# Feed-forward tiles in pairs: the orders of VectorE, ScalarE and GpSimd written anew over a whole pair, no operation moved between engines

## The chip, the cores and the metric

The kernel is one program on one core of a Trainium2 chip. Its metric is the device time of that core in microseconds. Engines are named as in the profile: PE is TensorE's matmul, PEld its weight load, DVE is VectorE, ACT ScalarE, POOL GpSimd, SP SyncE, which issues most DMAs. "L953" is line 953 of the kernel.

## What is computed

The input x is 4 x 2048 rows of 256. Three layers follow each other: half a feed-forward layer, causal attention with one head, and the same feed-forward layer again:

```python
x = x + 0.5 * ffn(layernorm(x), w_gate, w_up, w_down)
x = x + attention(layernorm(x), Wq, Wk, Wv)
x = x + 0.5 * ffn(layernorm(x), w_gate, w_up, w_down)

def fp4_linear(x, w):                      # einsum('bsk,nk->bsn')
    return fp4_quant_dequant(x) @ fp4_quant_dequant(w).T
def ffn(x, w_gate, w_up, w_down):          # inner width 704
    h = silu(fp4_linear(x, w_gate)) * fp4_linear(x, w_up)
    return fp4_linear(h, w_down)
```

`fp4_quant_dequant` takes blocks of 16 elements: scale = max|x| / 6, x / scale is rounded to the grid 0, 0.5, 1, 1.5, 2, 3, 4, 6 with its sign, and multiplied by the scale. It is applied to x (256 wide) and to h (704 wide), for every row. Attention is softmax over the scaled, causally masked scores, 2048 keys.

## The kernel before

The 8192 rows are 64 tiles of 128 rows, which stay in SBUF (`x_sb`). A feed-forward stage runs over 32 pairs of tiles; with `NP` = 32, a pair is `gp`, its tiles are 2 gp (`u` = 0) and 2 gp + 1 (`u` = 1). In the prediction they are called a and a+1. Between the two feed-forward stages lies attention. The order of every engine is written out by hand, as one function per engine that emits one pair (`pe_pair`, `dve_pair`, `act_pair`, `pool_pair`, `sp_pair`); loops repeat them, with pairs unrolled at both ends of a stage. Engines meet through semaphores that count tiles or pairs. Every engine works strictly in its order, and a wait holds up all that stands behind it.

What is done for a tile n of h, with the helpers' names and lines:

- TensorE: `pe_gate_up` (L1456, 18 matmuls) makes gate and up in PSUM for tile n, then `pe_down` (L1417, 17 matmuls) the down product of tile n-4. Before a gate and up product it waits for h of tile n-2, before a down product for the landing of the transposed codes of its tile and for the residual add two tiles back.
- ScalarE: `act_silu` (L708), `act_h_n` (L715, cells of the scaled h), `act_h_c` (L721, codes), `act_h_fc` (L725, a factor per row).
- VectorE: `dve_h` (L953, up times silu), `dve_h_amax` (L957, maxima of blocks), `dve_h_s` (L962, scales), `dve_h_rin` (L966, their reciprocals), `dve_h_max`, `dve_h_pow`, `dve_h_inv` (L970, L974, L979: one value per row), `dve_h_sp` (L984, scaled scales), `dve_h_sd`, `dve_h_sh`, `dve_h_sl` (L988, L992, L996: the scale split in a high and a low half), `dve_h_g` (L1001, rounding), `dve_h_q` (L1009, both code planes), `dve_res` (L1019, residual add, four tiles behind).
- GpSimd: `pool_h_y` (L540), h times the reciprocals of `dve_h_rin`.
- SyncE: `sp_h_T` transposes the code planes by DMA.

For a pair of x tiles, two to four pairs ahead: row statistics on ScalarE (`act_x_mean` L669, `act_x_squares` L681) and GpSimd (`pool_x_rstd`, three instructions of two elements, L515, L519, L521), normalised x (`act_x_z`, L693), and the same quantization: `dve_x_amax` L902, `dve_x_s` L907, `dve_x_rin` L911, `dve_x_sd`, `dve_x_sh`, `dve_x_sl` (L915, L919, L923), `pool_x_y` L529, `act_x_n` L702, `act_x_c` L730, `dve_x_g` L931, `dve_x_q` (L942, twice), and the transposition `sp_x_T`.

In `dve_pair` before, the body is a loop over u: each half begins with `dve_h_rin(n)`, then come h_max, the residual add, h_pow, h and h_amax of the next tile, h_inv, h_sp, h_q of the tile before, and the splitting of the scales. The x steps of pair gp+2 stand in the first half, those of gp+3 in the second. At the start of the second feed-forward stage two attention adds (`dve_last_add`, L1123, L1125, L1129) are still to be done; the stage's first down product waits for them (`o_add`), since it writes the PSUM bank that they read.

## Time and profile before

| | us |
|---|---|
| median of 3 runs | 1306.32 |
| lowest, highest | 1304.23, 1306.85 |
| the profiled execution | 1305.19 |
| its span, first to last instruction | 1303.4 |
| PE busy in the span | 1165.0 (89%) |
| DVE busy | 1054.2 (81%) |
| ACT busy | 786.9 (60%) |
| POOL busy | 568.9 (44%) |

The profile is of one execution; its span lacks 1.8 us of its time. Busy time counts an instruction from its start to its end, with what it waits for inside, so a group with a longer mean than its work explains is worth a look. The shares are means over stages: the first feed-forward stage runs from about 50 to 450 us, attention to about 920, and the second feed-forward stage to the end. In the timeline, "[0.35 <-issue]" is idle time of the engine before the instruction, and what ended it. TensorE's granted clock is 0.99 of full speed.

### The profile page before, as it was taken

Reading aid. Unit: us, or ns where it says so; the run is one execution under the profiler, and the core shown is the slowest. Engines: PE = TensorE matmul, PEld = TensorE weight load, DVE = VectorE, ACT = ScalarE, POOL = GpSimd, SP = SyncE. Lnnn points to the kernel's source line nnn. Section 1 sums busy time; section 2 is a strip of 40 time slices with the busy share of each in tenths; the row PEclk is TensorE's granted clock in tenths of the full one; section 3 lists DMA queues with packets and bytes.
Section 4 is the critical chain, followed back from the end, with each engine's and each line's share of the span. In section 5 each row is a group of like instructions: output and inputs, shape, how many; then the busy total and the mean of one; then the engine's idle time right before and its main releaser. Section 6 shows DMA issues by size and latency. Waiting matters only on the chain.

```text
span 1303.4 us, 25349 instructions
## 1 busy us (share of the span) xinstructions
PE 1165.0 (89%) x7673; PEld 746.1 (57%) x7673; DVE 1054.2 (81%) x3257; ACT 786.9 (60%) x1663; POOL 568.9 (44%) x531
## 2 busy tenths in 40 slices
PE   2689998998998789989998999989999889889897
PEld 1255555555554556666675667556665555555555
DVE  6899999999999766547555655664899999999997
ACT  4667777667764345435533543565676776776763
POOL 2444444544544244434442453444354454444442
PEclk9899999999999999999999999999999999999999
DMA  6953443444444546655663665556254454544545
GB/s 213 228 103 72 84 86 73 88 81 79 83 80 73 105 93 118 99 114 96 110 122 79 117 97 121 91 97 113 55 105 102 104 107 96 107 103 96 112 100 126
DMA packets 462743, 134.41 MB, mean 103 GB/s; under 512 B 441296, under 2 KB 461904, under 8 KB 462672
## 3 DMA queue, kind: packets, MB, share of 16 engines
q1 hardware_dynamic: 454928, 125.62, 50.1%
q10 hardware_dynamic: 7744, 7.86, 1.9%
q8 instruction: 42, 0.69, 0.2%
q14 instruction: 29, 0.24, 0.1%
HBM read 11.34 MB, written 8.39 MB: 15 GB/s over the span
## 4 chain that ended last, share of the span: by engine, by line
DVE 34%; PE 26%; issue 23%; ACT 8%; POOL 6%; DMA 1%; SPq 1%; ACTq 1%; DVEq 1%; POOLq 0%
PE ps L1503 11%; PE ps L1491 8%; DVE arena L953 5%; DVE arena L1009 5%; DVE arena L957 4%; POOL arena L540 3%; PE ps L1456 3%; POOL arena L529 2%; PE ps L1476 2%; DVE arena L1113 2%; DVE arena L966 2%; ACT arena L669 2%; PE ps L1469 1%; ACT arena L781 1%; DVE arena L942 1%
## 5 line engine op out<-in xcount | busy, mean ns | idle before, releaser
L1456 PE MATMUL ps<-wguT,arena 128*128 128x512 f16 (+1 forms) x2304 | 480.3, 363 | 5.7 <-DMA arena<-arena 5.6
L1456 PEld LDWEIGHTS ps<-wguT,arena 128*128 128x128 f16 x2304 | 225.9, 98 | 227.0 <-issue 10.3
L540 POOL TENSOR_TENSOR arena<-arena 128x704 f32<-128x704 f32 x128 | 192.0, 1500 | 368.3 <-DVE arena L966 368.3
L1417 PE MATMUL ps<-wdT,arena 128*128 128x256 f16 x2176 | 263.0, 275 | 73.1 <-DMA arena<-arena 69.4
L1417 PEld LDWEIGHTS ps<-wdT,arena 128*128 128x128 f16 x2176 | 209.4, 99 | 128.8 <-issue 74.1
L567 POOL TENSOR_TENSOR arena<-arena 128x128 f16<-128x128 f32 (+7 forms) x64 | 143.9, 2249 | 236.4 <-ACT arena L781 197.1
L715 ACT ACTIVATE arena<-arena 128x704 int16<-128x704 f32 x128 | 100.9, 788 | 167.0 <-POOL arena L540 165.9
L790 ACT ACTIVATE arena<-ps,arena,cst 128x128 f16<-128x128 f32 (+7 forms) x64 | 80.5, 1258 | 193.8 <-DVE arena L1118 189.9
L1503 PE MATMUL ps<-arena 128*128 128x256 f16 x1632 | 188.8, 273 | 9.3 <-DVE x_sb L1129 9.3
L1491 PE MATMUL ps<-arena 128*128 128x512 f16 (+3 forms) x960 | 187.7, 348 | 3.5 <-ACT arena L781 3.5
L1503 PEld LDWEIGHTS ps<-arena 128*128 128x128 f16 x1632 | 158.0, 98 | 37.0 <-DVE x_sb L1129 9.1
L1491 PEld LDWEIGHTS ps<-arena 128*128 128x128 f16 x960 | 91.2, 98 | 91.3 <-ACT arena L781 4.5
L953 DVE SCALAR_TENSOR_TENSOR arena<-ps,cst,arena 128x704 f32<-128x704 f32 x128 | 120.8, 944 | 23.1 <-issue 14.4
L1100 DVE SCALAR_TENSOR_TENSOR arena<-ps,arena 128x512 f16<-128x512 f32 x64 | 44.0, 691 | 98.7 <-ACT arena L773 98.7
L957 DVE TENSOR_REDUCE arena<-arena 128x44 f32<-128x704 f32 x128 | 113.4, 886 | 4.4
L708 ACT ACTIVATE arena<-ps,cst 128x704 f32<-128x704 f32 x128 | 106.6, 833 | 14.4 <-PE ps L1456 8.8
L1009 DVE TENSOR_TENSOR arena<-arena 128x1408 f16<-128x1408 f16 x128 | 113.4, 886 | 0.6 <-issue 0.3
L1113 DVE TENSOR_REDUCE arena<-ps 128x1 f32<-128x512 f32 (+3 forms) x160 | 95.2, 607 | 16.6 <-PE ps L1491 14.4
L721 ACT ACTIVATE arena<-arena 128x704 f16<-128x704 int16 x128 | 99.8, 779 | 0.4
L529 POOL TENSOR_TENSOR arena<-arena 128x512 f32<-128x512 f32 x64 | 69.6, 1087 | 55.5 <-DVE arena L911 55.5
L781 ACT ACTIVATE arena<-ps,arena,cst 128x128 f32<-128x128 f32 (+7 forms) x64 | 80.0, 1251 | 9.9 <-POOL arena L567 9.9
L1129 DVE SCALAR_TENSOR_TENSOR x_sb<-ps,arena,x_sb 128x256 f32 (+1 forms) x64 | 31.0, 484 | 58.3 <-PE ps L1503 53.7
(128 smaller groups left out, 1510.2 us busy)
## 6 DMA issues: line engine op xcount, KB each, us to landing
out_dram<-x_sb SPq DMA_DIRECT2D x32, 256.0 KB, 2.7
x_sb<-in_L_attn_x_dram ACTq DMA_DIRECT2D x3, 2048.0 KB, 8.7
arena<-arena SPq DMA_TRANSPOSE x384, 3.5
arena<-arena SPq DMA_DIRECT2D x8, 256.0 KB, 3.3
arena<-arena SPq DMA_DIRECT2D x4, 512.0 KB, 3.3
x_sb<-in_L_attn_x_dram ACTq DMA_DIRECT2D x1, 1536.0 KB, 7.3
arena<-in_L_ffn_w_down_dram SPq DMA_DIRECT2D x1, 704.0 KB, 8.8
arena<-in_L_ffn_w_gate_dram SPq DMA_DIRECT2D x1, 640.0 KB, 4.5
```

The costliest lines, as they stand in the source:

```text
L540: g.tensor_tensor(hy[u].rearrange("p (j b) -> p b j", j=BL), h[u].rearrange("p (b j) -> p b j", j=BL), hri[u].unsqueeze(2).to_broadcast([P ...
L567: nc.gpsimd.tensor_tensor(pq[k][1][:, 0:w], prob[:, 0:w], pq[k][0][:, 0:w], ALU.subtract).then_inc(p_lo, 1)
L708: nc.scalar.activation(sg[u], ps_gate[u], ACT.Silu, scale=cst[:, C_G:C_G + 1]).then_inc(h_silu, 1)
L715: nc.scalar.activation(hn[u], hy[u], ACT.Copy, scale=CELLS, bias=-0.5).then_inc(h_n, 1)
L953: V.scalar_tensor_tensor(h[u], ps_up[u], cst[:, C_U:C_U + 1], sg[u], ALU.mult, ALU.mult).then_inc(h_h, 1)
L957: V.tensor_reduce(ham[u], h[u].rearrange("p (b j) -> p b j", j=BL), axis=AX.X, op=ALU.max, apply_absolute_value=True).then_inc(h_amax, 1)
L1009: V.tensor_tensor(hq[u].rearrange("p (l j b) -> p l j b", l=2, j=BL), hc[u].rearrange("p (j b) -> p j b", j=BL).unsqueeze(1).to_broadcast( ...
L1113: m = V.tensor_reduce(scmax[:, c:c + 1], ps_s[:, c0 + c * GW:c0 + end], axis=AX.X, op=ALU.max)
L1417: i = nc.tensor.matmul(ps_dn[w % 2], hT[w][:, c * P:(c + 1) * P], wdT[:, k, :], start=(s == 0), stop=(s == len(DOWN_STEPS) - 1))
L1456: i = nc.tensor.matmul(psf[:, 1536 * u + lo:1536 * u + hi], xv[:, u, xl, kt, :], wguT[:, wl, lo // P:hi // P, kt, :], start=(s == 0), stop ...
L1491: m = nc.tensor.matmul(ps_s[:, c0:c0 + w], y[:, k, yl, qc:qc + P], zT[:, k, zl, k0:k0 + w], start=(s == 0), stop=(s == KT * 3 - 1))
L1503: m = nc.tensor.matmul(ps_o, pT[color(i)][pl][:, k, :], vs[:, vt, vl, :], start=(s == 0), stop=(s == len(steps) - 1))
```

## The change

The same operations are issued by the same engines. `dve_pair` no longer has a loop over u but one list for both tiles; `act_pair` and `pool_pair` are written anew too. `pool_x_rstd` is split in three functions so that its parts can stand apart. Two waits are added: `act_h_fc(n)` for the residual add of tile n-4, and `dve_h_pow(n)` for `act_h_fc(n-2)`. TensorE's and SyncE's orders are as before. The two attention adds of the second stage's second pair stand at new places.

```diff
         def pool_pair(gp, odd, x3=True, x4=True, z1=False):
             pool_h_y(2 * gp, 0)
+            if x4:
+                pool_x_var(gp + 4, odd)
             if z1:
                 pool_z_lo(1)
             pool_h_y(2 * gp + 1, 1)
+            if x4:
+                pool_x_root(gp + 4)
+                pool_x_shift(gp + 4, odd)
             if x3:
                 pool_x_y(gp + 3)
-            if x4:
-                pool_x_rstd(gp + 4, odd)
...
         def act_h_fc(n, u, w):
             nc.scalar.wait_ge(h_pw, n + 1)
+            if not isinstance(n, int) or n >= 4:
+                nc.scalar.wait_ge(res, n - 3)
...
         def act_pair(gp, p, odd, start=None, x2=True, x3=True, x4=True, z1=False):
+            a = 2 * gp
+            act_silu(a, 0)
+            if x4:
+                act_x_mean(gp + 4, p + 4, odd)
+            if start != 0:
+                act_h_n(a - 1, 1)
+                act_h_c(a - 1, 1)
+            act_silu(a + 1, 1)
...
+            if x2:
+                act_x_n(gp + 2)
+            if start != 0:
+                act_h_fc(a - 1, 1, (2 * odd - 1) % 4)
+            if x4:
+                act_x_squares(gp + 4, p + 4, odd)
+            if x2:
+                act_x_c(gp + 2)
+            if x3:
+                act_x_z(gp + 3, p + 3)
+            act_h_n(a, 0)
+            act_h_fc(a, 0, 2 * odd)
+            act_h_c(a, 0)
...
         def dve_h_pow(n, u):
             V.wait_ge(h_mx, n + 1)
+            if not isinstance(n, int) or n >= 2:
+                V.wait_ge(h_fc, n - 1)
...
+            a = 2 * gp
+            dve_h_rin(a, 0)
+            dve_h_max(a, 0)
+            dve_h(a + 1, 1)
+            if start is None:
+                dve_res(a - 4, 2 * odd, p * 2 - 4)
+            if adds:
+                dve_last_add(TB - 2)
+            dve_h_pow(a, 0)
+            dve_h_amax(a + 1, 1)
+            if start != 0:
+                dve_h_q(a - 1, 1, quad(qd, 2 * odd - 3))
+            if x2:
+                dve_x_sh(gp + 2)
+            dve_h_s(a + 1, 1)
+            if x2:
+                dve_x_sl(gp + 2)
+            dve_h_inv(a, 0)
+            dve_h_rin(a + 1, 1)
+            if x2:
+                dve_x_g(gp + 2)
+            dve_h_max(a + 1, 1)
+            dve_h_sp(a, 0)
+            if x3:
+                dve_x_amax(gp + 3)
+            if not end:
+                dve_h(a + 2, 0)
+            if x3:
+                dve_x_s(gp + 3)
+            dve_h_sd(a, 0)
+            if x2:
+                dve_x_q(gp + 2, 0, (qd + odd, 1 - odd))
+                dve_x_q(gp + 2, 1)
+            if x3:
+                dve_x_rin(gp + 3)
+            dve_h_pow(a + 1, 1)
+            if not end:
+                dve_h_amax(a + 2, 0)
+            dve_h_inv(a + 1, 1)
+            if start is None:
+                dve_res(a - 3, 2 * odd + 1, p * 2 - 3)
+            if adds:
+                dve_last_add(TB - 1)
+            dve_h_sp(a + 1, 1)
+            dve_h_sh(a, 0)
+            dve_h_sd(a + 1, 1)
+            dve_h_g(a, 0)
+            if not end:
+                dve_h_g(a + 1, 1)
+            dve_h_sh(a + 1, 1)
+            dve_h_sl(a, 0)
+            dve_h_sl(a + 1, 1)
+            dve_h_q(a, 0, quad(qd, 2 * odd - 2))
+            if not end:
+                dve_h_s(a + 2, 0)
+            if x3:
+                dve_x_sd(gp + 3)
```

**VectorE in the steady loop, where the second tile's reciprocals are made.** In the changed kernel the lines are higher by 22 to 24: L966 is L988, L970 is L992, L984 is L1008, L902 is L924, L907 is L929, L953 is L975, L931 (x_g) is now L953. Before, the second half of the pair begins:

```order
L966 RECIPROCAL arena<-arena 128x44
L901 REGISTER_ALU
L902 TENSOR_REDUCE arena<-arena 128x32
L970 TENSOR_REDUCE arena<-arena 128x1
L907 TENSOR_SCALAR arena<-arena 128x32
L1016 REGISTER_ALU
L1019 ISA
L1019 SCALAR_TENSOR_TENSOR x_sb<-ps,arena,x_sb 128x256
L911 RECIPROCAL arena<-arena 128x32
L974 TENSOR_SCALAR arena<-arena 128x1
L949 REGISTER_ALU
L953 SCALAR_TENSOR_TENSOR arena<-ps,cst,arena 128x704
```

and in the changed kernel:

```order
L988 RECIPROCAL arena<-arena 128x44
L953 TENSOR_SCALAR arena<-arena 128x512
L992 TENSOR_REDUCE arena<-arena 128x1
L1008 TENSOR_SCALAR arena<-arena 128x44
L923 REGISTER_ALU
L924 TENSOR_REDUCE arena<-arena 128x32
L971 REGISTER_ALU
L975 SCALAR_TENSOR_TENSOR arena<-ps,cst,arena 128x704
L929 TENSOR_SCALAR arena<-arena 128x32
L1012 SCALAR_TENSOR_TENSOR arena<-arena 128x44
```

Behind the reciprocals stood x_amax, h_max and x_s; now stand x_g, h_max and h_sp of the first tile (L1008), and x_s (L929) comes behind x_amax and h.

**VectorE in the second pair of the second feed-forward stage, where the last attention add stands** (three instructions, L1123 to L1129, now L1160 to L1166). Before:

```order
L966 RECIPROCAL arena<-arena 128x44
L902 TENSOR_REDUCE arena<-arena 128x32
L970 TENSOR_REDUCE arena<-arena 128x1
L907 TENSOR_SCALAR arena<-arena 128x32
L1123 RECIPROCAL arena<-arena 128x1
L1125 TENSOR_SCALAR arena<-arena,cst 128x1
L1129 SCALAR_TENSOR_TENSOR x_sb<-ps,arena,x_sb 128x256
L911 RECIPROCAL arena<-arena 128x32
L974 TENSOR_SCALAR arena<-arena 128x1
L953 SCALAR_TENSOR_TENSOR arena<-ps,cst,arena 128x704
```

and in the changed kernel, from h of the stage's tile 4 (L975) on:

```order
L975 SCALAR_TENSOR_TENSOR arena<-ps,cst,arena 128x704
L929 TENSOR_SCALAR arena<-arena 128x32
L1012 SCALAR_TENSOR_TENSOR arena<-arena 128x44
L964 TENSOR_TENSOR arena<-arena 128x2x256 x2
L933 RECIPROCAL arena<-arena 128x32
L998 TENSOR_SCALAR arena<-arena 128x1
L979 TENSOR_REDUCE arena<-arena 128x44
L1003 TENSOR_SCALAR arena<-arena 128x1
L1160 RECIPROCAL arena<-arena 128x1
L1162 TENSOR_SCALAR arena<-arena,cst 128x1
L1166 SCALAR_TENSOR_TENSOR x_sb<-ps,arena,x_sb 128x256
```

The add stood ahead of h (L953); now h (L975) and eight more steps stand ahead of it.

## Rows read from the trace of the kernel before

**Rows 1.** Stage table, two steady stretches: start:end length, busy us (count) per engine, clock, DMA.
```profile
89.07:379.71 290.64, 266.89 (x1701) 164.22 (x1700) 280.00 (x889) 211.34 (x530) 137.09 (x144) 1.00 0.43 81
950.89:1254.30 303.41, 278.19 (x1773) 171.03 (x1771) 292.07 (x927) 220.22 (x550) 142.86 (x150) 1.00 0.49 103
```

**Rows 2.** Timeline of one pair: start, us, engine, line, operation, shape, count [idle before <-releaser].
```profile
202.49 0.29 DVE L931 TENSOR_SCALAR arena<-arena 128x512 int16<-128x512 int16 x1
...
202.89 3.73 PE L1456 MATMUL ps<-wguT,arena 128*128 128x512 f16 x18
...
203.93 0.42 DVE L966 RECIPROCAL arena<-arena 128x44 f32<-128x44 f32 x1
...
204.43 1.49 POOL L540 TENSOR_TENSOR arena<-arena 128x704 f32<-128x704 f32 x1 [4.29 <-DVE arena L966]
...
204.93 1.02 DVE L907 TENSOR_SCALAR arena<-arena 128x32 f32<-128x32 f32 x1
205.77 0.47 DVE L1019 SCALAR_TENSOR_TENSOR x_sb<-ps,arena,x_sb 128x256 f32 x1
...
206.44 0.94 DVE L953 SCALAR_TENSOR_TENSOR arena<-ps,cst,arena 128x704 f32<-128x704 f32 x1
206.46 2.02 PE L1417 MATMUL ps<-wdT,arena 128*128 128x256 f16 x17
...
207.41 0.89 DVE L957 TENSOR_REDUCE arena<-arena 128x44 f32<-128x704 f32 x1
...
208.21 0.14 DVE L979 TENSOR_SCALAR arena<-arena 128x1 int32<-128x1 int32 x1
...
208.31 3.73 PE L1456 MATMUL ps<-wguT,arena 128*128 128x512 f16 x18
208.39 0.25 DVE L984 TENSOR_SCALAR arena<-arena 128x44 f32<-128x44 f32 x1
...
210.48 0.14 DVE L970 TENSOR_REDUCE arena<-arena 128x1 f32<-128x44 f32 x1
210.49 0.83 ACT L708 ACTIVATE arena<-ps,cst 128x704 f32<-128x704 f32 x1
...
211.42 0.95 DVE L953 SCALAR_TENSOR_TENSOR arena<-ps,cst,arena 128x704 f32<-128x704 f32 x1 [0.35 <-issue]
```

**Rows 3.** Line L907 over the whole kernel: minimum/median/maximum ns, first to last start.
```profile
L907 DVE TENSOR_SCALAR arena<-arena x64: 170/1027/1049, 23.7 to 1260.7; 128x32 f32<-128x32 f32 x64
```

**Rows 4.** Timeline, end of the first feed-forward stage, no x_s left.
```profile
436.46 1.49 POOL L540 TENSOR_TENSOR arena<-arena 128x704 f32<-128x704 f32 x1 [1.08 <-DVE arena L966]
...
437.11 0.88 DVE L984 TENSOR_SCALAR arena<-arena 128x44 f32<-128x44 f32 x1
```

**Rows 5.** Timeline, same stage, a GpSimd difference of 1024 columns beside VectorE.
```profile
432.51 2.87 POOL L558 TENSOR_TENSOR arena<-arena 128x1024 f16<-128x1024 f32 x1 [0.97 <-ACT arena L759]
432.51 0.89 DVE L1009 TENSOR_TENSOR arena<-arena 128x1408 f16<-128x1408 f16 x1
433.31 2.13 DVE L988 SCALAR_TENSOR_TENSOR arena<-arena 128x44 f32<-128x44 f32 x1
```

**Rows 6.** Timeline, start of the second feed-forward stage.
```profile
931.41 0.20 DVE L1123 RECIPROCAL arena<-arena 128x1 f32<-128x1 f32 x1
...
931.92 0.48 DVE L1129 SCALAR_TENSOR_TENSOR x_sb<-ps,arena,x_sb 128x256 f32<-128x256 f32 x1
...
934.02 0.95 DVE L953 SCALAR_TENSOR_TENSOR arena<-ps,cst,arena 128x704 f32<-128x704 f32 x1 [1.35 <-PE ps L1456]
...
934.03 2.02 PE L1417 MATMUL ps<-wdT,arena 128*128 128x256 f16 x17
```

**Rows 7.** Lines view, VectorE, 100 to 390 us: busy us, mean ns of one, idle before.
```profile
L942 DVE TENSOR_TENSOR arena<-arena 128x512 f16<-128x512 f16 x48 | 20.2, 421 | 0.0
...
L988 DVE SCALAR_TENSOR_TENSOR arena<-arena 128x44 f32<-128x44 f32 x48 | 9.5, 198 | 0.0
...
L911 DVE RECIPROCAL arena<-arena 128x32 f32<-128x32 f32 x24 | 8.1, 336 | 0.0
```

More of the change, by code:

```diff
@@ L508, in _, with pool_x_var @@
             sp.wait_ge(stored, 16 * NP)
-        def pool_x_rstd(q, par):
+        def pool_x_var(q, par):
             g = nc.gpsimd
@@ L515, in pool_x_rstd, with pool_x_root @@
             g.tensor_tensor(xve, xsq[par], eps_col[:, GT:GT + 2], ALU.add).then_inc(x_ve, 1)
+        def pool_x_root(q):
+            g = nc.gpsimd
             g.wait_ge(x_ve, q + 1)
@@ L519, in pool_x_rstd, with pool_x_shift @@
             g.tensor_tensor(xr, xve, half_neg[:, 0:2], ALU.pow).then_inc(x_rstd, 1)
+        def pool_x_shift(q, par):
+            g = nc.gpsimd
             g.wait_ge(x_rstd, q + 1)
             g.tensor_tensor(xnr, xnm[par], xr, ALU.mult).then_inc(x_nr, 1)
+        def pool_x_rstd(q, par):
+            pool_x_var(q, par)
+            pool_x_root(q)
+            pool_x_shift(q, par)
         def pool_x_y(q):
@@ L732, in act_pair @@
         def act_pair(gp, p, odd, start=None, x2=True, x3=True, x4=True, z1=False):
-            for u in range(2):
-                n, late = 2 * gp + u, start != 0 or u == 1
-                act_silu(n, u)
-                if u == 1 and z1:
-                    act_z_hi(1)
-                    act_load_table(ACT.Exp)
-                if u == 1 and x3:
-                    act_x_z(gp + 3, p + 3)
-                if late:
-                    act_h_n(n - 1, 1 - u)
-                if u == 0 and x2:
-                    act_x_n(gp + 2)
-                if u == 1 and x4:
-                    act_x_squares(gp + 4, p + 4, odd)
-                if late:
-                    act_h_c(n - 1, 1 - u)
-                    act_h_fc(n - 1, 1 - u, (2 * odd + u - 1) % 4)
-                if u == 0 and x2:
-                    act_x_c(gp + 2)
-                if u == 0 and x4:
-                    act_x_mean(gp + 4, p + 4, odd)
+            a = 2 * gp
[6 more added lines that the diff above has]
+            act_silu(a + 1, 1)
+            if z1:
+                act_z_hi(1)
+                act_load_table(ACT.Exp)
+            if x2:
[11 more added lines that the diff above has]
+            act_h_c(a, 0)
         def act_z_hi(g):
@@ L1023, in dve_last_add @@
             dve_attention_add((B - 1) * TB + i, i, ((B - 1) * TB + i) * D)
-        def dve_pair(gp, qd, p, odd, start=None, x2=True, x3=True, end=False, adds=()):
-            for u in range(2):
-                n, v, w = 2 * gp + u, 1 - u, 2 * odd + u
-                k = None if start is None else 2 * start + u
-                early, late = u == 0 and x2, u == 1 and x3
-                more = not (end and u == 1)
-                dve_h_rin(n, u)
-                if late:
-                    dve_x_amax(gp + 3)
-                dve_h_max(n, u)
-                if late:
-                    dve_x_s(gp + 3)
-                if k is None or k >= 4:
-                    dve_res(n - 4, w, p * 2 + u - 4)
-                for i, at_u in adds:
-                    if at_u == u:
-                        dve_last_add(i)
-                if late:
-                    dve_x_rin(gp + 3)
-                dve_h_pow(n, u)
-                if more:
-                    dve_h(n + 1, v)
-                    dve_h_amax(n + 1, v)
-                dve_h_inv(n, u)
-                if early:
-                    dve_x_sh(gp + 2)
-                dve_h_sp(n, u)
-                if k != 0:
-                    dve_h_q(n - 1, v, quad(qd, w - 3))
-                dve_h_sd(n, u)
-                if early:
-                    dve_x_sl(gp + 2)
-                    dve_x_g(gp + 2)
-                if late:
-                    dve_x_sd(gp + 3)
-                if more:
-                    dve_h_s(n + 1, v)
-                dve_h_sh(n, u)
-                if early:
-                    dve_x_q(gp + 2, 0, (qd + odd, 1 - odd))
-                if more:
-                    dve_h_g(n, u)
-                dve_h_sl(n, u)
-                if early:
-                    dve_x_q(gp + 2, 1)
@@ new lines, in dve_pair @@
+        def dve_pair(gp, qd, p, odd, start=None, x2=True, x3=True, end=False, adds=False):
+            a = 2 * gp
[55 more added lines that the diff above has]
+                dve_x_sd(gp + 3)
@@ L1381, in _ @@
                     wv_planes()
-                dve_pair(first + 1, first // 2, 1, 1, start=1, adds=((TB - 2, 0), (TB - 1, 1)) if first else ())
+                dve_pair(first + 1, first // 2, 1, 1, start=1, adds=(first > 0))
                 if not first:
```

## Prediction

> **What bounds the kernel now.** I first read the stage table for the two stretches of steady feed-forward work [rows 1]. The reader is to see that VectorE is busy 572.1 of 594.0 us, TensorE 545.1, ScalarE 431.6 and GpSimd 280.0, at full TensorE clock. The stretches hold 24 and 25 pairs of tiles, so a pair takes 12.12 us. Then I read the timeline of one pair [rows 2]. TensorE needs 3.57 us for a tile's gate and up product (202.89 to 206.46) and 1.85 for a down product (to 208.31): 10.84 per pair, less than the pair takes. VectorE sets the pace, yet it does not work all the time that it is called busy. Three losses stand in the rows:
>
> - **L907, blocked.** dve_x_s has 32 elements, and takes 1.02 us where GpSimd's product L540 (h_y) is under way (204.43 to 205.92); its end falls on that product's end. Over the kernel its shortest is 0.17 us and its median 1.03 [rows 3]. From its start to the next instruction are 0.84 us; unblocked, 0.17 less the overlap of 0.08 that neighbours show leaves 0.10. Loss 0.74 per pair.
> - **L953 of the next even tile** starts at 211.42, 0.10 behind the end of ScalarE's silu L708 (210.49 + 0.83). VectorE is idle for 0.35 before it, and unhindered it would also have had the overlap of 0.08. Loss 0.43.
> - **Back-to-back dependence.** L957 reads what L953 wrote and starts 0.03 behind its end (206.44 + 0.94 against 207.41). Independent neighbours start 0.08 before the end. That is 0.12 lost, twice per pair for L953 and L957, and once for L979 and L984 (208.21 + 0.14, then 208.39). Loss 0.36.
>
> Without them a pair would be 12.12 - 0.74 - 0.43 - 0.36 = 10.59 us of VectorE, below TensorE's 10.84.
>
> **The change, part by part.** No operation is added or removed, so only these losses and new ones count.
>
> *Dependence.* Every pair of dependent neighbours named above gets independent work in between (h_max before h, the residual add and h_pow between h and h_amax; h_inv and h_sp stand apart). All 0.36 go.
>
> *silu.* h of the odd tile now follows h_rin and h_max of the even tile directly, but its silu is issued far ahead: on ScalarE it stands before x_n, x_squares, x_c, x_z and h_n of the next tile. Laying the steps of the timeline end to end in the new order, I estimate that silu(a+1) is done some 3 us before h(a+1), and silu(a+2) 1.4 before h(a+2). The 0.43 go. On TensorE, by the same laying out, down(a) waits about 0.3 us for its transpose and down(a+1) about 0.5 for the residual add, which is placed later; both fit into the 0.8 us that TensorE has spare in a pair of 11.7.
>
> *x_s.* It stands behind x_amax and a whole h (0.54 + 0.86 us) after the product's start, by which time GpSimd is done. The 0.74 go.
>
> *The new stall.* GpSimd's second product, h_y(a+1), starts when h_rin(a+1) ends. In the new order VectorE then has x_g, h_max and h_sp of the even tile. h_sp is L984, and the rows show that it is stopped by the same product: 0.88 us [rows 4] instead of 0.25 [rows 2], ending 0.04 behind the product (436.46 + 1.49 against 437.11 + 0.88). h_y starts 0.08 after h_rin (203.93 + 0.42, then 204.43). h_sp can start only behind x_g (0.29) and h_max (0.14), each less 0.08: 0.18 after h_rin's end. GpSimd is 0.1 ahead. Nor does x_g's holding the port help: when L558 was held off by L1009 (2.87 us for its 1024 columns, both from 432.51), it was GpSimd that went on when L1009 ended, and L988, next in line, took 2.13 us until L558's end [rows 5]. So h_sp is stopped in every pair. Its successor x_amax starts about 0.15 before the product's end, as L1019 did (205.77 against 205.92): 0.08 + 1.50 - 0.15 = 1.43 behind h_rin. Free, it would start at -0.08 + 0.20 + 0.06 + 0.17 = 0.35 (L931's 0.29, L970's 0.14 and L984's 0.25 less 0.08 each). The new stall is 1.08. Its lower bound is 0 (VectorE gets the port first), its upper 1.16 (GpSimd starts 0.08 later, as it does behind some of its waits). I take 1.08, since L540 in the rows starts that way behind the same instruction.
>
> The Trainium skill, "SBUF — State Buffer", section Who interferes with whom, says that VectorE in a two-port mode, or with two SBUF inputs, and a reading GpSimd instruction exclude each other for a whole instruction, and that whoever issues first gets the pair. By that rule too GpSimd comes first here, and the trace agrees: L907 ends 0.03 behind the product.
>
> *The other products.* h_y(a) runs while VectorE does h_max, h, the residual add, h_pow and h_amax, which the rows show running beside L540 or reading PSUM; it ends some 0.4 us before h_q(a-1). x_y ends about when h_sp(a+1) starts: 0 to 0.1. I take 0 for both. x_var, x_root and x_shift act on two elements; split up, they run beside h_amax and h.
>
> *Sum for a pair:* 10.59 + 1.08 = 11.67, so 0.45 saved. It holds in the 49 pairs of the rows and about one more: 50 x 0.45 = 22.5 us.
>
> *Start of the second stage.* The last attention add moves behind h(4), x_s, h_sd, both x_q, x_rin, h_pow, h_amax and h_inv. h(4) starts at 934.02 because its product was late [rows 6]; that stays. From there the steps, each its duration in [rows 2] or [rows 7] less the overlap, are 0.86 + 0.10 + 0.11 + 0.34 + 0.34 + 0.25 + 0.01 + 0.80 + 0.06 = 2.87 (h_pow, of one element, all but vanishes under its neighbours), so the add starts at 936.89 and, taking 0.99 (931.41 to 931.92 + 0.48), ends at 937.88. The stage's first down product, which started at 934.03, waits for it: 3.9 us later, and behind it on TensorE the product of tile 5, whose h comes 3.9 later too. VectorE makes up none of it, since it goes on at 11.67 a pair from there. Cost 3.9, bounds 3 and 4.6.
>
> *Last pairs of each stage.* They have no x_s to gain from, but still the new stall (1.08 in one pair, and h_sd stopped for the rest of a product in the two that follow), against 0.36 saved in each. TensorE covers part of it. The start of the first stage I price at nothing: there is no attention add in it, and its first down product waits for transposed weights. Cost 1 per stage, bounds 0 and 2; together 2.
>
> Sum: -22.5 + 3.9 + 2 = -16.6 us. The profiled execution took 1305.19 us (1.8 outside its span), 1.1 less than the median of 1306.32. From the median: 1289.7; I say **1289**.
>
> **A rule that speaks against the change.** The rows show 0.12 us for each dependent neighbour. The Trainium skill, "VectorE: DVE Perf Modes", section The DRAIN you can't avoid, says that the next instruction waits for an empty pipe anyway and that a semaphore between costs nothing more. By it the 0.36 would not go, and the pair would be 12.03. The rows speak otherwise, so I count 0.36 and keep the rule as a rival.
>
> **The rivals.**
> 1. *VectorE gets the port first.* Then the pair is bounded by TensorE's 10.84: 1.28 x 50 = 64 saved, less 6: about 1248. For it: the race is 0.1 us wide. Against it: the handover to GpSimd in [rows 5]. Chance 0.07.
> 2. *Spacing dependent instructions brings nothing.* Each instruction then costs the same wherever it stands, and the losses are only renamed. Pair 12.03, 50 x 0.09 = 4.5 saved, 5.9 lost: 1307.7, no change. It is also about where the kernel would land if the silu wait stayed (0.43). Against it: the steps in [rows 2]. Chance 0.05.
> 3. *ScalarE's new order is late: slower.* h_fc(a-1) now waits for the residual add of tile a-3, and x_squares, x_c, x_z, h_n and h_c queue behind it. x_g, and with it the second half of the pair, waits for x_c. By my laying out x_c is done about 3.6 us before x_g. From 3.6 us of delay on, every further 0.1 costs 5 us over 50 pairs; at 4.2 the result would be 1289 + 30 = 1319. Against it: ScalarE is busy 8.8 of 12.1 us [rows 1], and the add comes about 0.6 us before h_fc. Chance 0.05.
>
> **How the numbers follow.** The forecast has 0.83. Its own range is 1283 to 1296: 0.08 later starts of h_y give +4, the start and the tails -3 to +3, and the many steps of 0.02 that I left out -3. What is left of the range, 1279 to 1299, is for errors in the count of pairs. It leaves out rival 1 on one side and rivals 2 and 3 on the other, 0.17 in all. A measurement tells 0.2% (2.6 us) from no change. Faster: 0.83 + 0.07 = 0.90; same: rival 2, 0.05; slower: rival 3, 0.05.
>
> **What would show it.** Right: the pairs at 11.6 to 11.75 us; dve_x_s at 0.18 us; h_sp with two forms, about 1.4 to 1.5 us for the even tile of a pair and 0.25 for the odd one; no idle time before h for silu; L953's successor no longer at +0.03; the down product of tile 0 in the second stage near 938. Wrong: h_sp at 0.25 throughout and TensorE without gaps (rival 1); steps between independent neighbours as long as between dependent ones (rival 2); idle time before x_g that ScalarE ends (rival 3); or a product of GpSimd that stops h_q or x_q, which I priced at nothing.

## The result, and the profile after

| | before | after |
|---|---|---|
| median of 7 runs each, us | 1304.23 | 1299.18 |
| lowest, highest | 1303.37, 1306.85 | 1296.09, 1301.17 |
| profiled execution, span | 1305.19, 1303.4 | 1299.57, 1297.7 |

The ratio after to before is 0.9952, 95% interval 0.9938 to 0.9966. The change is faster by 5 us (0.5%), where 17 were forecast. In the changed kernel's page, these lines answer to what the prediction watched: VectorE and TensorE, h, and h_sp.

```profile
PE 1177.7 (91%) x7673; PEld 745.0 (57%) x7673; DVE 1057.6 (81%) x3257; ACT 799.6 (62%) x1663; POOL 522.3 (40%) x531
...
L975 DVE SCALAR_TENSOR_TENSOR arena<-ps,cst,arena 128x704 f32<-128x704 f32 x128 | 121.0, 945 | 21.4 <-PE ps L1493 14.9
...
L1008 DVE TENSOR_SCALAR arena<-arena 128x44 f32<-128x44 f32 x128 | 105.6, 825 | 0.1
```

h_sp (L1008) takes 825 ns in the mean, where the same instruction took 0.25 us in the steady pair of before [rows 2]. The stage table of the changed kernel has the two steady stretches, and then two short ones at the start of the second stage (start:end length, busy us of PE, PEld, DVE, ACT, POOL, clock, DMA):

```profile
91.85:372.45 280.60, 269.08 (x1690) 161.24 (x1687) 280.60 (x890) 219.40 (x533) 117.36 (x144) 1.00 0.46 84
954.50:1246.81 292.31, 280.25 (x1765) 168.78 (x1763) 292.31 (x927) 227.74 (x550) 122.30 (x150) 1.00 0.52 107
928.00:936.00 8.00, 4.08 (x23) 1.99 (x22) 3.88 (x14) 3.11 (x7) 1.06 (x1) 1.00 0.60 114
936.00:943.00 7.00, 7.00 (x36) 3.94 (x35) 2.56 (x12) 0.78 (x2) 1.50 (x1) 0.76 0.34 63
```

The same 24 and 25 pairs as in [rows 1] now take 280.60 and 292.31 us, 11.69 a pair, and VectorE is busy without a break. The forecast for a pair was 11.67. So the steady work is as predicted, and the missing gain is elsewhere. Cut at the same pairs (a pair begins with the reciprocals of its first tile, L966 before and L988 after), the two profiled spans differ like this:

| stretch | before | after | difference |
|---|---|---|---|
| start of the program to pair 3 | 89.07 | 91.85 | +2.78 |
| 24 steady pairs | 290.64 | 280.60 | -10.04 |
| pair 27 | 13.82 | 13.40 | -0.42 |
| pair 28, over attention, to pair 0 of the second stage | 518.73 | 522.58 | +3.85 |
| its pairs 0 to 2 | 38.63 | 46.07 | +7.44 |
| 25 steady pairs | 303.41 | 292.31 | -11.10 |
| the last pairs | 49.08 | 50.93 | +1.85 |
| sum | 1303.38 | 1297.74 | -5.64 |

Steady pairs give 21.6 us, and four short stretches take 15.9 of them back. This is one execution of each kernel. The 24 steady pairs repeat well in the three kernels below that leave them as they are (280.57 to 280.63 us), but the first row does not: of its 2.78, 0.3 stand ahead of the first pair (its reciprocals start at 51.57 before and 51.88 after), and in two kernels below that are the same as the changed one up to there, pair 3 starts at 91.95 and 90.08.

**In a steady pair** the timeline of the changed kernel shows the stall where the prediction put it (an instruction is called stopped when it has started and is held until GpSimd's ends):

```profile
200.76 0.42 DVE L988 RECIPROCAL arena<-arena 128x44 f32<-128x44 f32 x1
...
201.09 0.23 DVE L953 TENSOR_SCALAR arena<-arena 128x512 int16<-128x512 int16 x1
201.24 0.18 DVE L992 TENSOR_REDUCE arena<-arena 128x1 f32<-128x44 f32 x1
201.26 1.51 POOL L554 TENSOR_TENSOR arena<-arena 128x704 f32<-128x704 f32 x1 [2.04 <-DVE arena L988]
201.34 1.46 DVE L1008 TENSOR_SCALAR arena<-arena 128x44 f32<-128x44 f32 x1
...
202.60 0.67 DVE L924 TENSOR_REDUCE arena<-arena 128x32 f32<-128x512 f32 x1
...
203.20 0.93 DVE L975 SCALAR_TENSOR_TENSOR arena<-ps,cst,arena 128x704 f32<-128x704 f32 x1
...
204.06 0.16 DVE L929 TENSOR_SCALAR arena<-arena 128x32 f32<-128x32 f32 x1
...
206.45 0.23 DVE L1008 TENSOR_SCALAR arena<-arena 128x44 f32<-128x44 f32 x1
```

GpSimd's product (L554) starts 0.08 behind the reciprocals, h_sp 0.085 behind that, and it ends 0.04 behind the product. So it is in every steady pair: h_sp starts 83 to 87 ns behind the product. x_amax (L924) starts at 202.60; the odd tile's h_sp takes 0.23. h (L975) has no idle time before it, and x_s (L929) takes 0.16 where it took 1.02 [rows 2].

**At the start of the second stage** the changed kernel's timeline has, for the attention adds and TensorE (L1540 is the product of attention weights and values, L1454 the down product):

```profile
921.15 0.95 DVE L975 SCALAR_TENSOR_TENSOR arena<-ps,cst,arena 128x704 f32<-128x704 f32 x1 [0.97 <-PE ps L1493]
...
922.45 0.48 DVE L1166 SCALAR_TENSOR_TENSOR x_sb<-ps,arena,x_sb 128x256 f32<-128x256 f32 x1
...
923.00 5.41 PE L1540 MATMUL ps<-arena 128*128 128x256 f16 x48 [1.89 <-DVE x_sb L1166]
928.25 3.73 PE L1493 MATMUL ps<-wguT,arena 128*128 128x512 f16 x18
...
932.05 0.95 DVE L975 SCALAR_TENSOR_TENSOR arena<-ps,cst,arena 128x704 f32<-128x704 f32 x1 [4.64 <-PE ps L1493]
...
935.35 0.48 DVE L1166 SCALAR_TENSOR_TENSOR x_sb<-ps,arena,x_sb 128x256 f32<-128x256 f32 x1
...
935.89 2.98 PE L1454 MATMUL ps<-wdT,arena 128*128 128x256 f16 x17 [3.92 <-DVE x_sb L1166]
938.66 4.50 PE L1493 MATMUL ps<-wguT,arena 128*128 128x512 f16 x18
```

Three things stand here. TensorE waits 3.92 us for the last add, as predicted (3.9). It also waits 1.89 for the add before it, which now stands behind an h (921.15) that waits for the end of its gate and up product. And behind the second gap its products are long: 2.98 us where a down product took 2.02 [rows 6], 4.50 where a gate and up product took 3.73 [rows 2]; the granted clock of 936 to 943 is 0.76 of full speed, so a part of that stretch was at 1.2 GHz. In before the same two stretches have 1.00.

**At the start of the first stage** SyncE's issues in before:

```profile
56.91 1.23 SPq L371 DMA_TRANSPOSE arena<-arena  x1
58.24 8.47 SPq L474 DMA_TRANSPOSE wdT<-arena  x6
66.75 3.15 SPq L378 DMA_TRANSPOSE arena<-arena  x2
```

and in the changed kernel:

```profile
59.62 1.23 SPq L371 DMA_TRANSPOSE arena<-arena  x1
60.96 7.89 SPq L474 DMA_TRANSPOSE wdT<-arena  x6
68.89 3.16 SPq L378 DMA_TRANSPOSE arena<-arena  x2
```

L371 transposes the codes that x_q makes of x pair 2. It stands ahead of the last six transposes of the down weights (L474) and of the first h codes (L378) on SyncE's queue. In the new order x_q of pair 2 stands in the second half of pair 0, behind h of the next pair's first tile, so L371 is issued 2.7 us later and L378 2.1, and the first down product starts at 72.67 instead of 70.52. In both kernels it starts 0.13 us behind the landing of the first h codes (70.39 and 72.54); the last down weights had landed 2.3 us before that.

### The profile page after: what moved, and what is told of

Read it like the earlier page. It is cut to its first block, busy times and chain, and to the rows that moved or that the text cites. A ratio compares the mean times of both kernels' runs of the same rounds, so it can differ in the third digit from the quotient of the medians.

```text
span 1297.7 us, 25574 instructions
## 1 busy us (share of the span) xinstructions
PE 1177.7 (91%) x7673; PEld 745.0 (57%) x7673; DVE 1057.6 (81%) x3257; ACT 799.6 (62%) x1663; POOL 522.3 (40%) x531
## 4 chain that ended last, share of the span: by engine, by line
PE 31%; DVE 31%; issue 19%; POOL 7%; ACT 7%; DMA 2%; SPq 2%; ACTq 1%; DVEq 1%; POOLq 0%
PE ps L1540 12%; PE ps L1528 9%; POOL arena L554 6%; DVE arena L1008 6%; PE ps L1493 5%; PE ps L1454 3%; ACT arena L725 2%; DVE arena L1150 2%; PE ps L1513 2%; DVE arena L1025 2%; DVE arena L924 2%; DVE arena L964 2%; DVE x_sb L1043 2%; PE ps L1506 1%; DMA arena<-arena 1%
## 5 line engine op out<-in xcount | busy, mean ns | idle before, releaser
L554 POOL TENSOR_TENSOR arena<-arena 128x704 f32<-128x704 f32 x128 | 192.9, 1507 | 327.7 <-DVE arena L988 327.7
L1454 PE MATMUL ps<-wdT,arena 128*128 128x256 f16 x2176 | 265.6, 277 | 54.1 <-DVE x_sb L1043 23.8
L1454 PEld LDWEIGHTS ps<-wdT,arena 128*128 128x128 f16 x2176 | 206.8, 99 | 121.7 <-issue 40.5
L1540 PE MATMUL ps<-arena 128*128 128x256 f16 x1632 | 190.6, 274 | 11.1 <-DVE x_sb L1166 11.0
L1540 PEld LDWEIGHTS ps<-arena 128*128 128x128 f16 x1632 | 159.0, 98 | 39.9 <-DVE x_sb L1166 10.9
L975 DVE SCALAR_TENSOR_TENSOR arena<-ps,cst,arena 128x704 f32<-128x704 f32 x128 | 121.0, 945 | 21.4 <-PE ps L1493 14.9
L1008 DVE TENSOR_SCALAR arena<-arena 128x44 f32<-128x44 f32 x128 | 105.6, 825 | 0.1
```

Source lines behind the costliest of these rows:

```text
L554: g.tensor_tensor(hy[u].rearrange("p (j b) -> p b j", j=BL), h[u].rearrange("p (b j) -> p b j", j=BL), hri[u].unsqueeze(2).to_broadcast([P ...
L975: V.scalar_tensor_tensor(h[u], ps_up[u], cst[:, C_U:C_U + 1], sg[u], ALU.mult, ALU.mult).then_inc(h_h, 1)
L1008: V.tensor_scalar(hsp[u], hs[u], hin[u], None, ALU.mult).then_inc(h_sp, 1)
L1454: i = nc.tensor.matmul(ps_dn[w % 2], hT[w][:, c * P:(c + 1) * P], wdT[:, k, :], start=(s == 0), stop=(s == len(DOWN_STEPS) - 1))
L1540: m = nc.tensor.matmul(ps_o, pT[color(i)][pl][:, k, :], vs[:, vt, vl, :], start=(s == 0), stop=(s == len(steps) - 1))
```

## The experiments

Each is an edit of the changed kernel, but two that edit the kernel before (ScalarE's new order alone, and x_s moved out of the product's reach). Ratios are to the kernel before on the same chip; its medians there were 1303.62 to 1305.12.

### The attention adds put ahead

```diff
             dve_h_max(a, 0)
+            if adds:
+                dve_last_add(TB - 2)
             dve_h(a + 1, 1)
...
-            if adds:
-                dve_last_add(TB - 2)
...
+            if adds:
+                dve_last_add(TB - 1)
             if not end:
                 dve_h(a + 2, 0)
...
-            if adds:
-                dve_last_add(TB - 1)
```

> The changed kernel with the two attention adds of the second stage's second pair put ahead of the two h steps (add TB-2 before h(a+1), add TB-1 before h(a+2)). Theory A (the adds stand behind h steps that wait for silu, so that TensorE's last weighted values and first down product come late, and the clock falls in the gap): the stage's start gets 1.9 + 3.8 + 1.7 = 7.4 us shorter, the time goes from 1299.2 to about 1292, and TensorE has no gap of several us before the first down product. Rival B (the start is slower because the pairs there are bound by silu in the new order anyway): under 2 us gained. Steady pairs stay at 11.69 us.

Measured: 1292.30 us, ratio 0.9915 (0.9899 to 0.9932), 6.9 less than the changed kernel. From pair 0 to pair 4 of the second stage it takes 50.44 us, where the changed kernel takes 57.77 and before 50.75. Its timeline of TensorE:

```profile
921.25 5.41 PE L1540 MATMUL ps<-arena 128*128 128x256 f16 x48
926.50 3.73 PE L1493 MATMUL ps<-wguT,arena 128*128 128x512 f16 x18
930.36 2.02 PE L1454 MATMUL ps<-wdT,arena 128*128 128x256 f16 x17
```

and its stage table:

```profile
936.00:943.00 7.00, 7.00 (x52) 4.85 (x50) 7.00 (x20) 6.97 (x20) 3.91 (x5) 1.00 0.79 105
```

Both gaps are gone, the down product is back at 2.02 and the clock at 1.00, as theory A has it. The place of the two adds makes the whole 7.3 us, the slow clock included.

### h_sp behind h

```diff
             dve_h_max(a + 1, 1)
-            dve_h_sp(a, 0)
             if x3:
                 dve_x_amax(gp + 3)
             if not end:
                 dve_h(a + 2, 0)
+            dve_h_sp(a, 0)
```

> The changed kernel with h_sp of the pair's first tile moved behind h(a+2), so that it no longer stands behind GpSimd's product. Theory A (h_sp is stopped by GpSimd's product and by nothing else, and behind it TensorE is the next bound): L1008 0.25 us for all, a steady pair 10.84 to 10.95 us instead of 11.69, time about 1299 - 50 x 0.8 = 1259 us. Rival B (the product stops whatever reads two SBUF operands next, x_s or h_sd): pair 11.4 to 11.7 and another line with a long form. Rival C (h_sp is long for a reason of its own): it stays at 1.46 us and the pair at 11.69.

Measured: 1255.81 us, ratio 0.9637 (0.9621 to 0.9654). Theory A holds: the steady pair is 10.84, which is TensorE's own time for two tiles. Stage table, 24 pairs:

```profile
90.49:350.62 260.13, 260.13 (x1681) 164.33 (x1680) 258.70 (x890) 212.95 (x529) 122.18 (x144) 1.00 0.49 91
```

and timeline:

```profile
203.02 1.52 POOL L554 TENSOR_TENSOR arena<-arena 128x704 f32<-128x704 f32 x1 [2.02 <-DVE arena L988]
203.10 0.68 DVE L924 TENSOR_REDUCE arena<-arena 128x32 f32<-128x512 f32 x1
...
203.90 0.95 DVE L975 SCALAR_TENSOR_TENSOR arena<-ps,cst,arena 128x704 f32<-128x704 f32 x1
...
204.76 0.24 DVE L1008 TENSOR_SCALAR arena<-arena 128x44 f32<-128x44 f32 x1
```

x_amax and h run beside the product at their own length, and h_sp, now behind its end, takes 0.24. TensorE is busy without a break. So the one stall of h_sp is what held the changed kernel's pair at 11.69; its removal is worth 0.85 a pair, and not the whole 1.08, because TensorE then bounds.

### The first pair of the first stage in its old order

```diff
-                dve_pair(first, first // 2, 0, 0, start=0)
+                (dve_pair if first else dve_pair_old)(first, first // 2, 0, 0, start=0)
```

and the same for `act_pair` and `pool_pair`, the old functions being those of before.

> The changed kernel with only the first pair of the first feed-forward stage in the order of before, on VectorE, ScalarE and GpSimd. Theory A (x_q of that pair stands late in the new order, SyncE issues the six transposes of the down weights behind its transpose, so the first down product is 2.15 us late and the slow clock behind the gap adds to it): first down product back from 72.7 to about 70.5 us, time 2 to 3 us below 1299.2. Rival B (the start is longer because of the second and third pair): under 1 us gained.

Measured: 1297.67 us, ratio 0.9952 (0.9935 to 0.9969). L371 is issued at 56.10 and the first down product starts at 69.78. Pair 3 starts at 89.52, 2.3 earlier than in the changed kernel, but 1.1 of that the edit did not bring: this execution's first pair began earlier (50.77, against 51.88). Counted from the start of the first pair, the way to pair 3 took 37.49 us before, 39.97 in the changed kernel and 38.75 here. So 1.2 of 2.5 came back. By the same count the first down product starts 18.95 behind the first pair before, 20.79 in the changed kernel and 19.01 here: its delay is gone whole. What stays is slow clock: the next gate and up product took 4.48 us here, 3.92 in the changed kernel and 3.73 before. The place of the loss is shown. For the whole, the medians differ by 1.5 us and the two intervals are nearly the same, so no gain is shown.

### The last four pairs of each stage in their old order

```diff
-                    dve_pair(first + k, ...)
+                    (dve_pair_old if k >= NP - 4 else dve_pair)(first + k, ...)
```

and the same for `act_pair` and `pool_pair`.

> The changed kernel with the last four pairs of each feed-forward stage in the order of before, on VectorE, ScalarE and GpSimd. Theory A (the order of the last pairs is what makes the ends longer: h_sp and h_sd stopped with no x_s to gain from, codes and transposes of the last tiles late): from pair 28 of the first stage to pair 0 of the second 518.7 us instead of 522.6, the last four pairs and the drain 49.1 instead of 50.9, time 5 to 6 us below 1299.2. Rival B (the ends are longer because of what stands before them): under 2 us gained.

Measured: 1292.64 us, ratio 0.9909 (0.9892 to 0.9925). From pair 28 to the second stage it takes 518.29 (before 518.73, changed 522.58), and the last pairs 49.03 (49.08, 50.93). As theory A has it, both losses are those of the last pairs, and attention, between them, has no part in it. The changed kernel's timelines show where most of it arises in the first stage, first VectorE and GpSimd, then TensorE:

```profile
405.13 1.51 POOL L554 TENSOR_TENSOR arena<-arena 128x704 f32<-128x704 f32 x1 [2.20 <-DVE arena L988]
405.21 3.46 DVE L1008 TENSOR_SCALAR arena<-arena 128x44 f32<-128x44 f32 x1
406.50 2.13 POOL L572 TENSOR_TENSOR arena<-arena 128x1024 f16<-128x1024 f32 x1
```

```profile
395.88 2.02 PE L1454 MATMUL ps<-wdT,arena 128*128 128x256 f16 x17 [2.60 <-DVE x_sb L1043]
...
411.03 3.68 PE L1454 MATMUL ps<-wdT,arena 128*128 128x256 f16 x17 [2.63 <-DVE x_sb L1043]
```

In the last pairs of the first stage GpSimd also has two differences of 1024 columns (L572) for attention. The first of them, in pair 29, follows the product of h without a break, and h_sp is stopped by both, 3.46 us instead of 1.46. The residual add (L1043) stands behind h_sp, the next h, both x_q and h_amax, and comes at 410.41. The down product waits 2.63 us for it, where the same tile's waited 1.30 (for a DMA) before, and then takes 3.68 instead of 2.02; the clock of 410 to 415 is 0.66. In the pair before it the add came late too: the down product at 395.88 waits 2.60, where the same tile's waited 1.33 before and 0.75 in the run with the old order. The run with h_sp moved behind h shows how much of this is h_sp's: there the stretch takes 519.75, so 2.8 of the 3.85 are gone, but the last pairs take 50.76, so nearly all of the 1.85 in the second stage comes from another part of the order. Which one stays open.

### h_amax directly behind its h

```diff
             dve_h(a + 1, 1)
+            dve_h_amax(a + 1, 1)
...
-            dve_h_amax(a + 1, 1)
```

> The changed kernel with h_amax(a+1) directly behind h(a+1), so that one dependent neighbour comes back in each pair; nothing else. Theory A (a dependent neighbour costs 0.12 us, 0.03 behind the end instead of 0.08 before it): pair 11.69 + 0.12 = 11.81, time about 6 us longer than the changed kernel's 1299.2. Rival B (spacing brings nothing): pair 11.69, same time.

Measured: 1307.92 us, ratio 1.0034 (1.0021 to 1.0046). The steady pair is 11.82 instead of 11.69, as theory A has it. VectorE's timeline, at the place of the edit:

```profile
208.96 0.94 DVE L975 SCALAR_TENSOR_TENSOR arena<-ps,cst,arena 128x704 f32<-128x704 f32 x1
209.93 0.89 DVE L979 TENSOR_REDUCE arena<-arena 128x44 f32<-128x704 f32 x1
210.73 0.47 DVE L1043 SCALAR_TENSOR_TENSOR x_sb<-ps,arena,x_sb 128x256 f32 x1
```

h_amax starts 0.03 behind the end of h, its independent successor 0.09 before h_amax's end. The difference, 0.12, is what a pair lost (0.13). By the rule that the prediction cites from the Trainium skill, "VectorE: DVE Perf Modes", section The DRAIN you can't avoid, read as the prediction reads it, it would have been nothing; here the measurement decides against that reading. The same section adds that a next instruction which is not held starts earlier. 50 pairs make 6.5 of the 8.7 us. The rest is not in the steady pairs: in the profiled execution the stretch from pair 28 to the second stage is 3.6 longer (526.15), and the start 1.5 shorter. Why the long stretch grew was not tested.

### Before, with ScalarE's new order alone

`act_pair` and the two added waits are taken over; VectorE and GpSimd stay as in before.

```diff
+            if not isinstance(n, int) or n >= 4:
+                nc.scalar.wait_ge(res, n - 3)
...
+            if not isinstance(n, int) or n >= 2:
+                V.wait_ge(h_fc, n - 1)
```

> The kernel before with ScalarE's order alone replaced by the new one (and the two added waits). VectorE's and GpSimd's orders as before. Theory A (the 0.35 us idle before h of the odd tile, and the lost overlap, are ScalarE's order alone): the silu wait goes, a steady pair is 11.70 us instead of 12.12, x_s stays at 1.03 us, the stages' starts and ends stay as before, time about 1304 - 50 x 0.4 = 1284 us, that is below the changed kernel. Rival B (ScalarE's order pays only together with VectorE's): pair 12.0 us or more.

Measured: 1286.26 us, ratio 0.9862 (0.9845 to 0.9878): 12.9 us below the changed kernel, near theory A's 1284. The 24 and 25 steady pairs take 281.50 and 293.63 us, 11.73 and 11.75 a pair. VectorE's groups, 100 to 380 us (busy us, mean ns, idle before):

```profile
L958 DVE SCALAR_TENSOR_TENSOR arena<-ps,cst,arena 128x704 f32<-128x704 f32 x48 | 45.0, 937 | 0.0
...
L912 DVE TENSOR_SCALAR arena<-arena 128x32 f32<-128x32 f32 x24 | 24.7, 1028 | 0.0
```

The wait before h (L958) is gone; x_s (L912) is stopped as before, and a pair is 0.39 shorter. That is nearly the prediction's silu term (0.43) by itself, and nearly what the whole change gains in a pair (0.43). The new orders of VectorE and GpSimd therefore brought almost nothing of their own in steady state, 0.04 a pair. By the prediction's terms VectorE's saves 0.74 and 0.36 and pays 1.08. Its costs at the ends are absent here: 51.34 us from pair 0 to pair 4 of the second stage, 518.90 over attention, 49.01 at the end.

### Before, with x_s moved out of the product's reach

```diff
-                if late:
-                    dve_x_s(gp + 3)
...
                     dve_h(n + 1, v)
+                if late:
+                    dve_x_s(gp + 3)
+                if more:
                     dve_h_amax(n + 1, v)
+                if late:
+                    dve_x_rin(gp + 3)
```

x_rin, which stood behind the residual add, goes with it.

> The kernel before with x_s moved behind h of the next tile, and x_rin behind h_amax, so that x_s does not meet GpSimd's product; nothing else. Theory A (stalls are coupled: x_s is freed, 0.18 us, but x_rin is later, so GpSimd's x_y, ScalarE's x_n and with them its silu are later, on which VectorE already waits): pair 12.9 to 13.2 us, slower by up to 1 us per pair, time 1304 + 50 = 1350 us. Rival B (each stall is a loss by itself): pair 12.12 - 0.74 = 11.4 us, time 1268 us.

Measured: 1356.22 us, ratio 1.0401 (1.0383 to 1.0418), and 13.07 and 13.10 a pair, as theory A has it. VectorE in its timeline:

```profile
202.60 0.94 DVE L953 SCALAR_TENSOR_TENSOR arena<-ps,cst,arena 128x704 f32<-128x704 f32 x1
203.46 0.17 DVE L907 TENSOR_SCALAR arena<-arena 128x32 f32<-128x32 f32 x1
204.78 1.12 DVE L984 TENSOR_SCALAR arena<-arena 128x44 f32<-128x44 f32 x1
...
209.62 0.95 DVE L953 SCALAR_TENSOR_TENSOR arena<-ps,cst,arena 128x704 f32<-128x704 f32 x1 [1.01 <-PE ps L1457]
```

x_s takes 0.17 us, and the kernel is 4% slower. x_rin, and with it GpSimd's x_y (204.80 to 205.86), comes late. h_sp (L984) is now stopped by x_y, to 0.04 behind its end, and takes 1.12 us, though it starts 20 ns ahead of it (so it is in every second pair). ScalarE waits 1.92 us for x_y, then does its queue without a break up to the next silu (208.69 to 209.52), and h (L953) starts 0.10 behind that, after 1.01 us of idle time. The view names TensorE's product there, but it had ended at 208.83. A stall of VectorE can't be taken out as a term by itself: what is behind it shifts against GpSimd's products and ScalarE's queue.

### Three repairs together, and the old ends with them

h_sp behind h, the adds ahead, the first pair of the first stage in its old order; then, with them, the last four pairs of each stage in their old order too (the edits are those above).

> The changed kernel with three moves together: h_sp behind h(a+2), the attention adds ahead of the h steps, the first pair of the first stage in the order of before. Theory A (the three effects add): 1255.8 - 7 - 2 = 1247 us. Rival B (with TensorE as the bound a delay at the start is partly made up later): 1250 to 1254 us.

> The kernel of the three moves (1245.2 us), and the last four pairs of each feed-forward stage in the order of before as well. Theory A (the old ends are shorter by what they were shorter by beside the changed kernel, 4.3 us in the first stage and 1.9 in the second): about 1240 us. Rival B (with steady pairs at TensorE's 10.84 us, four old pairs of up to 12.12 us give back what the ends gain): 1243 to 1247 us.

Measured: 1245.19 us, ratio 0.9544 (0.9528 to 0.956), and 1243.50 us, ratio 0.9535 (0.9513 to 0.9557). Both have steady pairs of 10.84 and 49.8 us from pair 0 to pair 4 of the second stage. For the three moves this is 2 us less than theory A's 1247. The old ends take the last pairs from 51.56 to 49.06 and the stretch over attention from 520.28 to 519.34. Of this 3.4 us, 1.3 are given back where the old order begins (pair 27 and the 25 steady pairs, 0.7 and 0.6 longer), as rival B has it. The medians show 1.7, which the two intervals don't tell from nothing; 1240, theory A's time, was missed. These two versions are faster than both kernels, by some 60 us than before.

### Which instruction meets the product: h_sp first

```diff
+            dve_h_sp(a, 0)
+            dve_h_max(a + 1, 1)
             if x2:
                 dve_x_g(gp + 2)
-            dve_h_max(a + 1, 1)
-            dve_h_sp(a, 0)
```

> The changed kernel with h_sp(a) directly behind h_rin(a+1), and x_g behind h_max: rin, sp, max, x_g instead of rin, x_g, max, sp. Theory A (GpSimd takes the port some 0.1 to 0.2 us after h_rin's end, and then stops the first VectorE instruction that needs it): L1008 gets through at 0.25 us, x_g (L953) is stopped in its place at about 1.4 us, and the pair stays near 11.7 us; time 1296 to 1302 us. Rival B (only h_sp, with its operand per row, is stopped): pair 10.9 us or less, time below 1262 us.

Measured: 1253.59 us, ratio 0.9615 (0.9598 to 0.9632), 10.84 a pair.

```profile
203.11 0.15 DVE L1008 TENSOR_SCALAR arena<-arena 128x44 f32<-128x44 f32 x1
...
203.27 1.66 POOL L554 TENSOR_TENSOR arena<-arena 128x704 f32<-128x704 f32 x1 [2.03 <-DVE arena L988]
203.28 0.28 DVE L953 TENSOR_SCALAR arena<-arena 128x512 int16<-128x512 int16 x1
```

x_g (L953) starts 4 ns behind the product (203.278 and 203.274) and is not stopped; it is the product that takes 0.15 longer. So it is in all steady pairs, where x_g starts 3 to 7 ns behind and takes 280 to 286. Theory A is refuted: x_g is not stopped here. The pair is rival B's, but whether B's reason holds (that only h_sp, with its operand per row, can be stopped) this run can't tell; the next one does.

### Which instruction meets the product: x_g last

```diff
             dve_h_rin(a + 1, 1)
-            if x2:
-                dve_x_g(gp + 2)
             dve_h_max(a + 1, 1)
             dve_h_sp(a, 0)
+            if x2:
+                dve_x_g(gp + 2)
```

> The changed kernel with the order rin, max, sp, x_g: x_g behind both others. In the run with rin, sp, max, x_g, x_g starts 0.004 us behind GpSimd's product and gets through, while in the changed kernel h_sp starts 0.085 behind it and is stopped. Here h_sp starts before the product, and x_g by the steps (0.06 for max, 0.15 for sp) 0.05 us behind it. Theory A (whoever's start stands first has the port, up to a few ns): x_g is stopped, 1.4 us, pair 11.6 to 11.7 us, time 1294 to 1300 us. Rival B (GpSimd needs some 0.05 to 0.08 us after its start before it holds the port): x_g gets through, pair 10.84 us, time about 1254 us.

Measured: 1310.68 us, ratio 1.0044 (1.0027 to 1.006), 11.92 a pair.

```profile
203.80 0.23 DVE L1008 TENSOR_SCALAR arena<-arena 128x44 f32<-128x44 f32 x1
203.90 1.50 POOL L554 TENSOR_TENSOR arena<-arena 128x704 f32<-128x704 f32 x1 [2.03 <-DVE arena L988]
203.94 1.61 DVE L953 TENSOR_SCALAR arena<-arena 128x512 int16<-128x512 int16 x1
```

h_sp is free here, and x_g, 37 ns behind the product (35 to 39 in all steady pairs), is stopped until its end. So the last run's rival B had the wrong reason: x_g can be stopped as h_sp can, and whether it is depends on some 30 ns of its start. This kernel is slower than the changed one, beyond theory A's 1300: x_g ends 0.15 behind the product, where the stopped h_sp ended 0.04 behind, and x_amax starts 1.65 us behind h_rin's end instead of 1.43, which is the 0.23 that a pair is longer. Between h_rin and x_amax this kernel, the one with h_sp first and the changed one have the same three instructions, in three orders. The times are 1310.7, 1253.6 and 1299.2.

## Why the prediction was right or wrong

- **Dependence, silu, x_s (0.36, 0.43, 0.74): held.** Of the three dependent neighbours, one was put back (h_amax directly behind h) and cost 0.13 a pair, 0.12 predicted; the other two are argued from it. The silu wait alone gave 0.39 (ScalarE's order alone), and x_s takes 0.16 in the changed kernel. ScalarE's new order was not late: in the steady stretch nothing of VectorE waits for it.
- **The new stall (1.08): held.** h_sp took 1.46 us, and its successor started at 202.60, 1.42 behind h_rin's end (1.43 predicted). The Trainium skill's rule, "SBUF — State Buffer", section Who interferes with whom, that the one that issues first keeps the pair, agrees: 85 ns behind, h_sp ended 0.04 after the product. By starts of less than some 30 ns apart the traces don't bear the rule out, as the last section shows. The pair: 11.69 measured, 11.67 predicted. With 0.4 in pair 27 that is 21.6 us; 22.5 was forecast.
- **Start of the second stage (3.9): mis-sized, it was 7.4. This is the largest miss of the sum.** The step that failed is the one that counted only the last add. The wait for it was 3.92, as worked out. Missed was the add before it, which the change puts behind an h that waits for its gate and up product: 1.89 more. Missed too was that the clock falls behind the gap: the down product and the next gate and up product took 0.96 and 0.77 longer. 3.92 + 1.89 + 1.73 is 7.5, and putting the adds ahead gave 7.3 back.
- **Start of the first stage, "I price at nothing": wrong, about 2.5.** The reason given, that the first down product waits for transposed weights, names the wrong wait: it waits last for h codes (landing at 70.39 before, the weights at 68.08). Weights and h codes alike stand on SyncE's queue behind the transposition of x codes, and the change makes these later. The diff leaves SyncE's order alone, and the queue carried the delay all the same. With the old first pair the first down product's delay went whole, and 1.2 of the 2.5. The row of 2.8 has 0.3 from ahead of the first pair.
- **Last pairs (1 a stage, bounds 0 and 2): mis-sized, 3.85 and 1.85.** The old order of the last four pairs gave back 4.3 and 1.9. I counted h_sp's stall in one pair of each stage, at 1.08. It is stopped in two (at 390.56 and 405.21, and at 1251.08 and 1262.77). Left out was that a GpSimd difference for attention follows the product in the first stage, so that h_sp is stopped for 3.46 us, that the residual add behind it is then late for the down product (2.60 and 2.63 us of TensorE), and that the clock falls. With h_sp out of the way 2.8 of the 3.85 went, and 0.2 of the 1.85.
- **Rival 1: rightly not taken, and a repair overlooked.** GpSimd is first in every steady pair, by 83 to 87 ns, as the rows had it. But the rival's time for a pair, 10.84, is what the kernels reached in which h_sp met no product, and in one of them (h_sp first) only the order of three instructions decided. That the race was so near was to be read in the same rows, as a repair rather than a risk.

The result lies just above the range because the costs of the transitions were all too low: 5.9 us were put in for them, and 15.9 came. That the pair came within 0.02 has a little luck in it: the silu term was 0.04 too large, and what the rest brings was put 0.02 too low.

## What to carry to other kernels

After a reordering, price the first and last iterations of every stage as carefully as the steady one, and follow each moved step into the queues whose order the diff doesn't touch. Where two engines exclude each other, write down for each long product of one which instruction of the other starts within 0.1 us of it, and put there one that is not stopped. Test each engine's new order alone: here ScalarE's was worth more by itself (18 us) than the whole change (5).

## What the runs showed of the hardware

- **A race decided within some tens of ns.** x_g starting 4 ns behind GpSimd's product (3 to 7 in all steady pairs) is not stopped, and the product takes 1.66 us instead of 1.51; 1 ns behind, in before (432.506 and 432.507), it was GpSimd that took 2.87 [rows 5]. 37 ns behind (35 to 39) x_g is stopped to the product's end, and so is h_sp 85 ns behind (83 to 87). In each of these kernels the outcome is the same in every steady pair. None of them has a start between 7 and 35 ns.
- **The recorded start alone doesn't tell who wins.** With x_s moved, h_sp starts 20 ns ahead of GpSimd's x_y in every second steady pair and is stopped all the same (1.12 us, to 0.04 behind its end). In the pairs between it starts 100 ns ahead and takes its 0.25. There h_sp stands directly behind the instruction whose result it reads; whether that is the reason was not tested.
- **GpSimd's start behind a VectorE result has two values.** Before and after, its product starts 79 ns behind the reciprocals of a pair's second tile and 159 ns behind those of the first (78 to 79 and 158 to 160 over 22 pairs of the first stage). Why was not tested.
- **The clock falls behind a gap.** Behind TensorE's 3.9 us of idle time the next down product took 2.98 us here, and 3.81, 3.14, 3.47, 3.81 and 3.26 in five other kernels with the same gap, instead of 2.02. A gap of 2.63 was followed by 3.68 (clock 0.66 in 410 to 415), one of 2.60 in the same kernel by 2.02. At the start of the first stage, gaps of 5.86, 6.05 and 5.90 were followed by down products of 3.36, 3.78 and 3.79 and gate and up products of 3.73, 3.92 and 4.48, so the length of the gap alone doesn't tell what is lost. What else does stays open.
